# A six-stage float32 kernel: expert weights fetched per tile, or all held in SBUF and copied by VectorE and ScalarE

## What is computed

```python
# gated ("glu"), x is layer-normed before; out is added to x with factor 0.5
h = einsum('td,edh->eth', xf, W0) + b0[:, None, :]            # d 128, h 512
g = silu(einsum('td,edh->eth', xf, W1) + b1[:, None, :])
y = einsum('eth,ehd->etd', h * g, W2) + b2[:, None, :]
out = einsum('te,etd->td', combine, y)                        # combine: softmax of the top 2 gates
# ungated ("mlp")
h = gelu(flat @ W1[e] + b1[e]);  out = out + combine[:, e:e + 1] * (h @ W2[e] + b2[e])
```

## Time and profile before

| | us |
|---|---|
| median of 3 runs (lowest, highest) | 1119.5 (1117.77, 1120.09) |
| the profiled execution | 1118.18 |
| its span, first to last instruction | 1116.4 |

### The profile page before, as it was taken

One profiled execution on the slowest core, in us unless ns is written; L12 is line 12 of the kernel. 1 busy time (PEld: TensorE's weight loads), 2 busy tenths in 40 slices (PEclk: granted clock), 3 DMA queues, 4 the chain that ended last, 5 costly groups with the idle time before them and its releaser, 6 DMA issues.

```text
span 1116.4 us, 17251 instructions
## 1 busy us (share of the span) xinstructions
PE 797.7 (71%) x5220; PEld 680.7 (61%) x5220; DVE 538.7 (48%) x1633; ACT 445.3 (40%) x1259; POOL 433.3 (39%) x448
## 2 busy tenths in 40 slices
PE   0579997378989865899974767774177877777750
PEld 0479997267777645798973566664034555666650
DVE  4734444777656537344447521113889543310117
ACT  0045554144445320455550145553087331265540
POOL 1256663022222210565631066663453210466631
PEclk9999999698989985799995579997598885699995
DMA  4559985362513003598954247775000011477752
GB/s 110 131 177 293 291 271 180 95 152 55 124 42 82 2 9 121 179 291 279 276 174 132 94 114 213 211 207 144 1 0 1 1 30 35 136 212 211 210 162 65
DMA packets 79082, 153.77 MB, mean 138 GB/s; under 512 B 11082, under 2 KB 54035, under 8 KB 78992
## 3 DMA queue, kind: packets, MB, share of 16 engines
q1 hardware_dynamic: 69008, 134.03, 40.6%
q0 software_dynamic: 9984, 18.65, 6.1%
HBM read 134.21 MB, written 20.25 MB: 138 GB/s over the span
## 4 chain that ended last, share of the span: by engine, by line
PE 58%; DVE 24%; issue 7%; DMA 4%; ACT 3%; POOL 3%; SPq 1%; another core or an unknown queue 0%; POOLq 0%; ACTq 0%; DVEq 0%
PE bank L521 14%; PE bank L512 12%; PE bank L509 8%; PE bank L945 2%; DVE stats L281 2%; PE bank L528 2%; PE bank L460 2%; PE bank L935 2%; DVE oh_b L623 2%; PE bank L497 2%; DVE sh_tok L675 2%; PE bank L1270 2%; DVE x_tok L675 2%; PE bank L908 1%; PE bank L477 1%
## 5 line engine op out<-in xcount | busy, mean ns | idle before, releaser
L512 PE MATMUL bank<-xt,weights 128*128 128x128 f32 x1248 | 249.8, 283 | 27.5 <-ACT xt L411 16.6
L521 PE MATMUL bank<-hid,weights 128*128 128x128 f32 x1248 | 245.1, 279 | 11.0 <-ACT hid L422 8.2
L348 POOL DMA_INDIRECT xg<-xn_rows,gidx x156 | 153.1, 982 | 238.7 <-DVE gidx L629 129.9
L512 PEld LDWEIGHTS bank<-xt,weights 128*128 128x128 f32 x1248 | 196.5, 199 | 33.9 <-ACT xt L411 20.3
L521 PEld LDWEIGHTS bank<-hid,weights 128*128 128x128 f32 x1248 | 191.1, 194 | 15.3 <-ACT hid L422 9.5
L355 POOL DMA_INDIRECT y_rows<-yo,sidx x156 | 157.1, 1007 | 91.8 <-issue 56.3
L650 DVE SCALAR_TENSOR_TENSOR hid<-bank,weights,act_ring 128x128 f32<-128x128 f32 x312 | 108.9, 349 | 139.5 <-ACT act_ring L422 83.2
L422 ACT ACTIVATE act_ring<-bank,weights 128x128 f32<-128x128 f32 x312 | 115.8, 371 | 111.1 <-PE bank L512 96.5
L657 DVE COPY yo<-bank 128x128 f32<-128x128 f32 x156 | 44.6, 286 | 213.2 <-remote 127.6
L422 ACT ACTIVATE hid<-bank,weights 128x128 f32<-128x128 f32 x312 | 110.6, 372 | 79.8 <-PE bank L521 51.1
L509 PE MATMUL bank<-xt,weights 128*128 128x128 f32 x624 | 128.8, 289 | 5.8 <-issue 2.5
(11 more groups left out here) (220 smaller groups left out, 1341.8 us busy)
## 6 DMA issues: line engine op xcount, KB each, us to landing
weights<-glu_pack SPq DMA_DIRECT2D x78, 772.5 KB
weights<-mlp_pack SPq DMA_DIRECT2D x78, 514.5 KB
v_sb<-v_rows SPq DMA_DIRECT2D x48, 180.0 KB, 6.5
y_in<-y_rows SPq DMA_DIRECT2D x32, 256.0 KB, 5.0
xn_rows<-xm_tok SPq DMA_DIRECT2D x16, 256.0 KB, 2.2
v_rows<-vd SPq DMA_DIRECT2D x16, 256.0 KB, 2.8
xg<-xn_rows,gidx POOLq DMA_INDIRECT x156
y_rows<-yo,sidx POOLq DMA_INDIRECT x156
```

Of the source, the lines that this page charges most:

```text
L348: pool.indirect_dma_start(out=xg[:, slot, :], out_offset=None, in_=xn_dram.ap()[:, :], in_offset=bass.IndirectOffsetOnAxis(ap=gidx[:, j:j ...
L512: nc.tensor.matmul(banks[k % 4][:, 0:TS], wt[:, slot, o:o + P], xt[:, j % 2, :], start=True, stop=True).then_inc(sem(st + "_up"), 1)
L521: nc.tensor.matmul(YD[j % 2], wt[:, j % WSLOTS, o:o + P], hid[:, k % 4, :], start=c == 0, stop=c == HC - 1).then_inc(sem(st + "_dn"), 1)
```

## The change

Each MoE stage fetches the weights of all eight experts once, with three DMAs (biases, up, down), into all_w in SBUF, right behind the last xn_rows DMA. The experts of the tiles are packed eight to a word of 24 bits (te_word, 5 words), which TensorE, VectorE and in gated stages ScalarE load into registers. The stationary operands of the up products need an address that isn't from a register here: for each tile they are copied from all_w to one of four slots of wt, in gated stages the first 512 columns by ScalarE and 520 by VectorE, in ungated ones 516 by VectorE. wt lies over eq_a, oh_a and oh_b, so the copies wait for TABLE. The down product's operands change places: hid is stationary and the weights move, read from all_w by register. The result comes out token-major, so the transpose L528 and its copy L430 go, and VectorE adds the output bias from out_bias, rows made ahead of the loop by two products of ones_sq with diag. SP issues nothing in the tile loop.

```diff
-WSLOTS, XSLOTS, PIECES, LAG = 5, 6, 4, 3
+WSLOTS, XSLOTS, PIECES, LAG = 4, 6, 4, 3
+PACK = 8
+WORDS = -(-NTILE // PACK)
...
-        XT, YO = banks[6][:, 0:TS], banks[7][:, 0:TS]
+        YD = [banks[4][:, 0:D], banks[5][:, 0:D]]
+        XT = banks[6][:, 0:TS]
+        BIAS = banks[2:4]
...
-        te_f = sb("te_f", [1, NTILE])
-        te_i = sb("te_i", [1, NTILE], I32)
+        te_f = sb("te_f", [1, WORDS * PACK])
+        te_word = sb("te_word", [1, WORDS], F32)
+        te_i = sb("te_i", [1, WORDS], I32)
+        digit = sb("digit", [1, WORDS, PACK])
...
-        xm_tok, xT_sb, wt, eq_a, oh_a, oh_b, xg, xt, act_ring, hid, yt, yo, y_in, sh_tok, mix_w, cv_w = shared_place(
-            ("xm_tok", [P, NT, D], F32), ("xT_sb", [P, NBLK, BC], F32), ("weights", [P, WSLOTS, GLU_COLS], F32),
+        eq_a, oh_a, oh_b, xm_tok, xT_sb, all_w, xg, xt, act_ring, hid, yo, y_in, sh_tok, mix_w, cv_w = shared_place(
             ("eq_a", [P, 2 * NT, NA], F32), ("oh_a", [P, 2 * NT, NA], R32), ("oh_b", [P, 2 * NT, P], R32),
+            ("xm_tok", [P, NT, D], F32), ("xT_sb", [P, NBLK, BC], F32), ("all_w", [P, E * GLU_COLS], F32),
             ("xg", [P, XSLOTS, D], F32), ("xt", [P, 2, TS], F32), ("act_ring", [P, 4, TS], F32),
-            ("hid", [P, 4, TS], F32), ("yt", [P, 2, TS], F32), ("yo", [P, NTILE, D], F32),
+            ("hid", [P, 4, TS], F32), ("yo", [P, NTILE, D], F32),
             ("y_in", [P, 2, NT, D], F32), ("sh_tok", [P, NT, D], F32),
...
-        def tile_weights(sp, n, st, m, j):
-            slot = j % WSLOTS
-            pack = glu_pack if m.gated else mlp_pack
-            if j >= WSLOTS:
-                sp.wait_ge(sem(st + "_ysb"), st.at("_ysb", j - WSLOTS + 1))
-            e = sp.value_load(te_i[0:1, j:j + 1], min_val=0, max_val=E - 1)
-            sp.dma_start(wt[:, slot, 0:m.cols], pack[:, bass.ds(e * m.cols, m.cols)]).then_inc(
-                sem(st + f"_w_in{slot}"), 16)
+        def all_weights(sp, n, st, m):
+
+            pack = (glu_pack if m.gated else mlp_pack).rearrange("p (e c) -> p e c", e=E)
+            here = all_w[:, 0:E * m.cols].rearrange("p (e c) -> p e c", e=E)
+            up = m.ups * 512
+            for first, there, count in ((up, up + 512, m.down - up), (0, 0, up), (m.down, up, 512)):
+                sp.dma_start(here[:, :, first:first + count], pack[:, :, there:there + count]).then_inc(
+                    sem(st + "_weights_in"), 16)
+
+        def tile_words(eng, st, which=range(WORDS)):
+
+            eng.wait_ge(sem(st + "_te"), st.at("_te", 1))
+            return [eng.value_load(te_i[0:1, i:i + 1], min_val=0, max_val=E ** PACK - 1) for i in which]
+
+        def expert(words, j):
+            return (words[j // PACK] >> (3 * (j % PACK))) & (E - 1)
...
+            all_weights(sp, n, st, m)
             if feeds(n):
                 rwkv_raw(sp)
             if n == 0:
                 zero_values(sp)
-            sp.wait_ge(sem(st + "_te"), st.at("_te", 1))
-            for j in range(NTILE):
-                tile_weights(sp, n, st, m, j)
...
-            def tile_out(j):
-                act.wait_ge(sem(st + "_dn"), st.at("_dn", HC * (j + 1)))
-                if j >= 2:
-                    act.wait_ge(sem(st + "_yT"), st.at("_yT", j - 1))
-                act.activation(yt[:, j % 2, :], YD[j % 2], ACT.Identity,
-                               bias=wt[:, j % WSLOTS, m.bias_out:m.bias_out + 1]).then_inc(sem(st + "_ysb"), 1)
-
+            act.wait_ge(sem(st + "_rows"), st.at("_rows", 1))
+            for i in range(2):
+                act.activation(out_bias[:, 512 * i:512 * i + 512], BIAS[i][:, :], ACT.Copy).then_inc(
+                    sem(st + "_out_bias"), 1)
+            def tile_weights(j):
+
+                if j >= WSLOTS:
+                    act.wait_ge(sem(st + "_hid"), st.at("_hid", HC * (j - WSLOTS + 1)))
+                act.activation(wt[:, j % WSLOTS, 0:512], all_w[:, bass.ds(expert(words, j) * m.cols, 512)],
+                               ACT.Copy).then_inc(sem(st + "_tile_act"), 1)
+
+            if m.gated:
+                words = tile_words(act, st)
+                act.wait_ge(sem(st + "_table"), st.at("_table", 1))
+                act.wait_ge(sem(st + "_weights_in"), st.at("_weights_in", 16 * 3))
+                for j in range(WSLOTS - 1):
+                    tile_weights(j)
             tile_in(0)
             for j in range(NTILE):
                 chunk(j, 0)
@@ -437,10 +459,9 @@
                 if j + 1 < NTILE:
...
-                if j:
-                    tile_out(j - 1)
+                if m.gated and j + WSLOTS - 1 < NTILE:
+                    tile_weights(j + WSLOTS - 1)
                 chunk(j, 3)
-            tile_out(NTILE - 1)
...
+            words, first = tile_words(pe, st), [0, 0]
...
             ins.then_inc(sem(st + "_table"), 1)
+            pe.wait_ge(sem(st + "_diag"), st.at("_diag", 1))
+            if not m.gated:
+                pe.wait_ge(sem(st + "_shared_act"), st.at("_shared_act", NBLK))
+            for i in range(2):
+                ins = nc.tensor.matmul(BIAS[i][:, :], ones_sq[:, :],
+                                       diag[:, 4 * i:4 * i + 4, :].rearrange("p e d -> p (e d)"), start=True, stop=True)
+            ins.then_inc(sem(st + "_rows"), 1)
...
-                    pe.wait_ge(sem(st + f"_w_in{slot}"), st.at(f"_w_in{slot}", 16 * (j // WSLOTS + 1)))
+                    pe.wait_ge(sem(st + "_tile_w"), st.at("_tile_w", j + 1))
+                    if m.gated:
+                        pe.wait_ge(sem(st + "_tile_act"), st.at("_tile_act", j + 1))
...
-                    pe.wait_ge(sem(st + "_ysb"), st.at("_ysb", j - 1))
-                o = m.ups * 512 + c * P
-                nc.tensor.matmul(YD[j % 2], wt[:, j % WSLOTS, o:o + P], hid[:, k % 4, :],
+                    pe.wait_ge(sem(st + "_yo"), st.at("_yo", j - 1))
+                if c == 0:
+                    first[j % 2] = pe.snap(expert(words, j) * m.cols + m.down)
+                nc.tensor.matmul(YD[j % 2], hid[:, k % 4, :], all_w[:, bass.ds(first[j % 2] + c * P, P)],
                                  start=c == 0, stop=c == HC - 1).then_inc(sem(st + "_dn"), 1)
-
-            def tile_out(j):
-                pe.wait_ge(sem(st + "_ysb"), st.at("_ysb", j + 1))
-                if j:
-                    pe.wait_ge(sem(st + "_yo"), st.at("_yo", j))
-                nc.tensor.transpose(YO, yt[:, j % 2, :], ident[:, :]).then_inc(sem(st + "_yT"), 1)
...
-                    if c == 0 and j >= 2:
-                        tile_out(j - 2)
...
-            tile_out(NTILE - 2)
             for k in range(HC * NTILE - LAG, HC * NTILE):
                 down(k)
-            tile_out(NTILE - 1)
...
-            nc.vector.tensor_scalar_min(te_i[0:1, :], te_f[0:1, :], E - 1.0).then_inc(sem(st + "_te"), 1)
+            digits = te_f[0:1, :].rearrange("p (w d) -> p w d", d=PACK)
+            nc.vector.scalar_tensor_tensor(digits, digits, E - 1.0, digit[0:1, :, :], ALU.min, ALU.mult)
...
+            nc.vector.tensor_reduce(te_word[0:1, :], digits, AX.X, ALU.add)
             link(nc.vector.tensor_reduce(pos[:, :, :], place[:, :, :, :].rearrange("p k e t -> p k t e"), AX.X, ALU.add))
+            nc.vector.tensor_copy(te_i[0:1, :], te_word[0:1, :]).then_inc(sem(st + "_te"), 1)
...
+            words = tile_words(v, st, range(1))
+            v.wait_ge(sem(st + "_weights_in"), st.at("_weights_in", 16 * 3))
+            spread = [P, E, D]
+            biases = all_w[:, 0:E * m.cols].rearrange("p (e c) -> p e c", e=E)[:, :, m.bias_out:m.bias_out + 1]
+            nc.vector.tensor_tensor(diag, ident[:, :].unsqueeze(1).broadcast_to(spread), biases.broadcast_to(spread),
+                                    ALU.mult).then_inc(sem(st + "_diag"), 1)
...
+            def tile_weights(j):
+
+                slot = j % WSLOTS
+                if j >= WSLOTS:
+                    v.wait_ge(sem(st + "_hid"), st.at("_hid", HC * (j - WSLOTS + 1)))
+                first = v.snap(expert(words, j) * m.cols)
+                lo, hi = 512 * (m.ups - 1), m.bias_out
+                nc.vector.tensor_copy(wt[:, slot, lo:hi], all_w[:, bass.ds(first + lo, hi - lo)]).then_inc(
+                    sem(st + "_tile_w"), 1)
+
             def tile_out(j):
-                v.wait_ge(sem(st + "_yT"), st.at("_yT", j + 1))
-                nc.vector.tensor_copy(yo[:, j, :], YO).then_inc(sem(st + "_yo"), 1)
-
+                v.wait_ge(sem(st + "_dn"), st.at("_dn", HC * (j + 1)))
+                nc.vector.tensor_tensor(yo[:, j, :], YD[j % 2], out_bias[:, bass.ds(expert(words, j) * D, D)],
+                                        ALU.add).then_inc(sem(st + "_yo"), 1)
+
+            for j in range(WSLOTS - 1):
+                tile_weights(j)
+            words += tile_words(v, st, range(1, WORDS))
+            v.wait_ge(sem(st + "_out_bias"), st.at("_out_bias", 2))
             for j in range(NTILE):
                 for c in range(HC):
                     chunk(j, c)
```

(13 more changed lines are left out.)

17 lines of the change are left out of this document (7 added, 10 removed).

## The result

| | before | after |
|---|---|---|
| median of 20 runs each, us (lowest, highest) | 1117.45 (1114.3, 1120.09) | 1121.69 (1118.26, 1127.91) |
| the profiled execution, us (its span) | 1118.18 (1116.4) | 1127.91 (1126.1) |

A forecast was written before the change was run, and what follows sets the result against it. Bound: TensorE's passes (gated) and GpSimd's gather-scatter pair (ungated), plus pauses from SP's weight DMAs. Gains of 6.2, 4.8 and 30.8, together 41.8 us, took 1118.2 to 1076.4, as a median 1077.7; range 1056 to 1118.

The forecast's parts named there:

- A tile loses 0.25 us (gated) and 0.4 (ungated) to pauses: MoE tile loops: SP's weight DMAs cause pauses of that size per tile, which the change removes.
- Rival A: Tile loops: pauses stay, being GpSimd's scatter's doing; a tile saves only the transpose, 0.11 us; 1113.5 us, chance 0.12.
- the end of the stage: Evidence against GpSimd's scatters as cause: after the last weight fetch, scatters run without SP DMA and no pauses occur.
- Gated 2.85, gain 11.5 a stage: Gated tile: 25 TensorE passes, 2.78 us, plus 0.07 for registers; gain 10.5 us, and 1.0 at the stage's end.
- Ungated GpSimd pair of 2.64, gain 15.4: Ungated tile loop: GpSimd's gather and scatter repeat each 2.64 us; 20.4 us less charges, net 15.4 per stage.
- VectorE's copies lock GpSimd for 0.08 us each: Ungated loop: VectorE's weight copies delay GpSimd by 0 to 0.25 us, mean 0.08, 3 us a stage.
- rival B: Tile loops: each VectorE copy holds GpSimd for its whole 0.43 us; 1117.7 us, no change; chance 0.11.
- rival C: Tile loops: TensorE's register arithmetic is exposed, 1.2 us per tile; 1201 us; chance 0.15.
- the 0.5 us charged for routing: Before the tile loop: digit operations for packing experts lengthen the routing by 0.5 us in each stage.
- xt 8 us behind gidx: Gated stage's start: ScalarE's added work puts the first xt 8 us behind gidx; charged 3.8 and 5.2 us.
- Weights late by 1 us: Before the gated loops: fetching all weights ends 0 to 5 us late for diag; 1 us charged per gated stage.
- rival D: Before the gated loops: weights come late by 5 us or more per stage; 1087.7 us, inside the forecast's own range.

The follow-up runs named there:

- b_no_fetch: The kernel before with SP fetching weights for only the first five tiles of a stage; 1116.3 us, beside 1120.6 for the kernel before on that chip.
- a_direct_out: The changed kernel with the scatters taken out and SP storing the first 32 tiles of yo by plain DMAs; 1008.2 us.
- a_one_gather: The changed kernel with only the first six gathers of each stage, all scatters kept; 1016.1 us.
- a_again: The changed kernel, unaltered, run on another chip; 1115.2 us.
- a_no_copy_timed: The changed kernel with weight copies for the first four tiles of a stage only; 1111.4 us, ratio 1.0002 to the kernel before.
- a_late_words: The changed kernel with four of TensorE's five word loads inside the tile loop, ScalarE's words and weight copies before its bias-row wait; ratio 1.0005 to the kernel before.

## Why the prediction was wrong

- *A tile loses 0.25 us (gated) and 0.4 (ungated) to pauses*: the pauses are there, but this is the step that failed: "the span of silence holds SP's weight DMA" chose the wrong one of two neighbours. It was the scatter close behind the gather. b_no_fetch keeps the pause (3.23 and 3.19 us a gated tile), a_direct_out loses it (2.79). Rival A had this, and was put at 0.12 because of "the end of the stage": there only scatters are left, 2.9 us apart, which a_one_gather shows to be harmless, so that evidence spoke for neither. The other, "gathers alone at 650 to 655 with no such pause", holds for that stretch, but the trace of before had the counterexample: in the first stage, with gathers back to back and no fetch of SP near, the activation of 70.26 comes 2.1 us late. The timeline of before has it:

```profile
68.66 0.94 POOL L348 DMA_INDIRECT xg<-xn_rows,gidx  x1 [0.30 <-issue]
70.26 0.37 ACT L422 ACTIVATE act_ring<-bank,weights 128x128 f32<-128x128 f32 x1 [2.40 <-PE bank L512]
```

- *Gated 2.85, gain 11.5 a stage*: the term for TensorE, 25 passes, is right (2.79 wherever one DMA is alone), the tile stays at 3.20 and 3.26. The transpose that is gone saved nothing, as TensorE wasn't the bound while updates were held. Rival A charged it a gain of 0.11 a tile, which did not come either.
- *Ungated GpSimd pair of 2.64, gain 15.4*: GpSimd can do the pair in that, but does 25 in 80 us. The gain would have needed TensorE's updates to arrive beside back-to-back DMAs.
- *VectorE's copies lock GpSimd for 0.08 us each* (rival B: 0.43): nearer the former. On one chip scatters of 80 to 165 us take 1027 ns in the mean with copies (a_again) and 1012 without (a_no_copy_timed); in the middle of the ungated loops it is 1033 and 1034 against 1020 and 1017. So GpSimd's DMA is longer by 0.015 us, and the two ungated stages, charged 3 us each, are 0.9 and 2.0 us shorter without the copies.
  The Trainium skill (SBUF — State Buffer, § SBUF: two separate sides) has the shared port as a lock that whichever of the two begins first holds for its whole instruction, the other blocked until then. The prediction used only the half in which VectorE is first. This case agrees in part: gated copies that begin within a scatter take up to 0.71 us, but 17 of after's ungated ones lie wholly within a scatter and take 0.43, as if alone.
- *Register arithmetic* (rival C): false: with one indirect DMA a gated tile takes 2.79 us, its 25 passes at 0.111. But the five loads of words on TensorE, which the sum left out, kept it from its first one-hot product until 52.62, 3.7 us later than in a_late_words. That and the digits took the place of the 0.5 us charged for routing: gidx 1.3 us later than in the trace of before in the first stage (59.90 against 58.58; in b_no_fetch, the same routing on another chip, it is 57.4), and by the ratios 0.43% in all.
- *xt 8 us behind gidx*: right (8.1), priced at 3.8 and 5.2 us, cost nothing.
- *Weights late by 1 us* (rival D): diag starts within 0.1 us of the end of the last one-hot, at 55.50 and in the third stage at 452.30, so they are in time.

The sum's 41.8 us were 63.8 us of shorter tiles (11.5 and 20.4 a stage) less 22.0 of charges. Of the 63.8 nothing came; of the charges, the 9 us for xt cost nothing, and the head's 0.43% was missing but for 0.5 us a stage. (One slip besides: the 103.7 us of the ungated loop add up to 103.5 from their own terms, which changes nothing.) Copies and loads of words, at about 0.45% each by their ratios, come to more than the 0.48% by which after is slower, and would leave the change a saving of its own of some 0.4%; the intervals leave nearly all of that open, and no kernel had both taken out together.

## What to carry to other kernels

A pause that holds two suspects is not read by taking the nearer one: take each away, or find a stretch with each alone and with the other's load. Before crediting a shorter engine, find what the loop's period is made of; here it was the wait for a signal, and shortening TensorE, freeing SP and cutting the traffic to about a fifth moved nothing. Loads of registers belong where the engine has nothing due behind them.
